# A two-stage attention kernel: more of three fp16 splits moved between ScalarE, VectorE and GpSimd, and PSUM banks of Sx and of k/v alternated one by one

## What is computed

```python
qkv = einsum('bcxy,oc->boxy', gn(x), w_qkv)      # q, k, v: 8 images x 8 heads x 64 x 4096
context = einsum('ndm,nem->nde', softmax(k), v)
content_out = einsum('nde,ndm->nem', context, q)
Sx = einsum('ndxy,xid->nixy', q4, Px)
Yh = einsum('nixy,neiy->nexy', Sx, v4)           # then batch norm over images, rows, columns
Sy = einsum('ndxy,yid->nixy', q4, Py)
out = content_out + einsum('nixy,nexi->nexy', Sy, Yh)
x + einsum('bcxy,oc->boxy', out, w_out) + b_out
```

## Time and profile before

| | us |
|---|---|
| median of 3 runs | 2915.45 (2914.46 to 2922.74) |
| the profiled execution | 2908.83 |
| its span | 2907.0 |
| TensorE busy in the span | 2596.9 (89%) |
| VectorE | 2017.8 (69%) |
| ScalarE | 1689.4 (58%) |
| GpSimd | 1402.7 (48%) |

### The profile page before, as it was taken

The page is one execution under the profiler, slowest core; times in us unless marked ns, Lnnn a source line. Parts: engine busy times, 40 slices in busy tenths (PEclk is TensorE's granted clock), DMA queues, the critical chain, the costliest instruction groups (busy, mean ns, idle before and its releaser), DMA issues. The chain is left out here.

```text
span 2907.0 us, 119666 instructions
## 1 busy us (share of the span) xinstructions
PE 2596.9 (89%) x54900; PEld 2105.4 (72%) x54900; DVE 2017.8 (69%) x3126; ACT 1689.4 (58%) x2984; POOL 1402.7 (48%) x617
## 2 busy tenths in 40 slices
PE   4899999899899999999999996689899898989897
PEld 3787787787687787787777785667676767666674
DVE  7577677677667667667667655787677768677774
ACT  3655655655555565565565564566565656566563
POOL 0424424424434344334344343776766767676761
PEclk9999999999999999999999998799999999999999
DMA  2423523522532542532544335577768777777763
GB/s 99 128 72 82 156 62 88 144 68 75 141 83 68 132 99 69 141 90 68 127 104 119 94 87 121 133 196 194 186 179 229 177 207 172 214 194 197 187 172 109
DMA packets 448615, 382.35 MB, mean 132 GB/s; under 512 B 307312, under 2 KB 374128, under 8 KB 448112
## 3 DMA queue, kind: packets, MB, share of 16 engines
q1 hardware_dynamic: 429680, 341.14, 46.7%
q10 hardware_dynamic: 18432, 33.56, 3.2%
HBM read 205.79 MB, written 168.82 MB: 129 GB/s over the span
## 5 line engine op out<-in xcount | busy, mean ns | idle before, releaser
L843 POOL TENSOR_TENSOR k_f<-k_f,negmax 128x1024 f32<-128x1024 f32 x128 | 303.3, 2397 | 858.7 <-DVE negmax L810 858.7
L456 PE MATMUL bank<-w_hi,x_hi 128*128 128x256 f16 x2048 | 572.0, 279 | 11.0 <-DVE x_lo L735 7.7
L456 PE MATMUL bank<-w_hi,x_lo 128*128 128x256 f16 x2048 | 565.4, 276 | 3.8 <-issue 3.8
L456 PE MATMUL bank<-w_lo,x_hi 128*128 128x256 f16 x2048 | 566.2, 276 | 0.0
L1290 POOL TENSOR_TENSOR x_f<-x_f,ones 128x1024 f32<-128x1024 f32 x127 | 287.2, 2261 | 227.7 <-DMA x_f<-y_scratch 223.2
L1242 DVE TENSOR_TENSOR yb_lo<-x_f,yb_hi 64x1024 f16<-64x1024 f32 x192 | 367.5, 1914 | 31.8 <-ACT yb_hi L1156 28.8
L750 DVE TENSOR_TENSOR v_lo<-bank,v_hi 128x256 f16<-128x256 f32 x512 | 214.0, 421 | 249.5 <-ACT v_hi L598 246.7
L597 ACT ACTIVATE k_f<-bank 128x256 f32<-128x256 f32 x512 | 200.5, 392 | 289.1 <-PE bank L456 287.6
L456 PEld LDWEIGHTS bank<-w_hi,x_hi 128*128 128x128 f16 x2048 | 297.0, 145 | 22.5 <-issue 15.0
L456 PEld LDWEIGHTS bank<-w_lo,x_hi 128*128 128x128 f16 x2048 | 299.7, 146 | 2.3
L456 PEld LDWEIGHTS bank<-w_hi,x_lo 128*128 128x128 f16 x2048 | 297.5, 145 | 2.6
(11 more groups left out here) (152 smaller groups left out, 8312.7 us busy)
## 6 DMA issues: line engine op xcount, KB each, us to landing
y_scratch<-yst SPq DMA_DIRECT2D x256, 256.0 KB, 4.7
x_f<-y_scratch SPq DMA_DIRECT2D x256, 256.0 KB, 6.3
q<-q_scratch SPq DMA_DIRECT2D x256, 256.0 KB, 4.9
x_f<-x SPq DMA_DIRECT2D x64, 512.0 KB, 5.8
q_scratch<-q_hi SPq DMA_DIRECT2D x128, 256.0 KB
q_scratch<-q_lo SPq DMA_DIRECT2D x128, 256.0 KB
x_res<-x SPq DMA_DIRECT2D x128, 256.0 KB, 6.1
out<-x_res ACTq DMA_DIRECT2D x128, 256.0 KB, 4.2
```

The lines of the kernel that those rows point to most:

```text
L456: mm = pe.matmul(outs, lhs[a], rhs[m], start=first and n == 0, stop=last and n == 2, **kw)
L843: pool.tensor_tensor(kk, kk, negmax[:, :].unsqueeze(1).to_broadcast([P, 8, P]), ALU.add).then_inc(shifted, 1)
```

## The change

Three things are moved; the arithmetic stays the same.

1. In the alternating stretches of stage 1, sx and kv alternate one by one.
2. In the split of x, ScalarE casts both channel halves (L576 of the changed kernel in place of L571 and L715); VectorE only subtracts (L721). The last quarter's casts move from behind q 7 to behind sx 0 of head pair 3, and its two subtractions (VectorE, GpSimd) from behind yh 7 to behind sx 2.
3. In stage 2, at head pair 2 `yb_lo` of piece 2 is written by GpSimd too. At head pair 3 piece 2 is split (both halves) behind ro 0 of head pair 3 and no more behind ro 6 and 7 of head pair 2.

```diff
-                for i in range(0, SX, 2):
-                    order += [("sx", hp, i), ("sx", hp, i + 1), ("kv", hp + 1, i), ("kv", hp + 1, i + 1)]
+                for i in range(SX):
+                    order += [("sx", hp, i), ("kv", hp + 1, i)]
...
+            SPLIT_X_HI = {("q", HP - 1, 1): 0, ("q", HP - 1, 3): 1, ("q", HP - 1, 5): 2, ("sx", HP - 1, 0): 3}
+            SPLIT_X_LO = {("yh", HP - 2, 1): 0, ("yh", HP - 2, 3): 1, ("yh", HP - 2, 5): 2, ("sx", HP - 1, 2): 3}
...
                 def split_x(nth, piece):
-                    act.wait_ge(x_norm, nth * 8 + piece * CC + 1)
-                    act.activation(x_hi[:, 0, :, piece * XR:piece * XR + XR, :], x_piece(0, piece),
-                                   ACT.Copy).then_inc(x_hi_a, 1)
+                    for c, done in enumerate((x_hi_a, x_hi_b)):
+                        act.wait_ge(x_norm, nth * 8 + piece * CC + c + 1)
+                        act.activation(x_hi[:, c, :, piece * XR:piece * XR + XR, :], x_piece(c, piece),
+                                       ACT.Copy).then_inc(done, 1)
...
                     s = slice(j * XR, j * XR + XR)
-                    dve.wait_ge(x_norm, nth * 8 + (CC * j + 2))
-                    dve.tensor_copy(x_hi[:, 1, :, s, :], x_piece(1, j)).then_inc(x_hi_b, 1)
+                    dve.wait_ge(x_norm, nth * 8 + (CC * j + 1))
                     dve.wait_ge(x_hi_a, nth * NXC + (j + 1))
...
         LAST_SPLIT = {("ro", 0): ((3, 0),), ("ro", 1): ((3, 1),)}
-
-        LO_DVE = 2 * (YC - 1)
+        LAST_SPLITS = {("ro", 0): ((2, 0), (2, 1)), ("ro", 1): ((3, 0), (3, 1))}
+
+        def on_pool(hp, c):
+            return c == YC - 1 or (hp == 2 and c == YC - 2)
...
                             if i % 2 == 1:
                                 continue
-                            if i < RO - 2:
-                                pe.wait_ge(yb_lo_done, t * LO_DVE + (i + 2))
+                            if on_pool(hp, i // 2):
+                                pe.wait_ge(yb_lo_pool, lows(True, t, i // 2 + 1))
                             else:
-                                pe.wait_ge(yb_lo_pool, t * 2 + 2)
+                                pe.wait_ge(yb_lo_done, lows(False, t, i // 2 + 1))
```

More of the change, by code:

```diff
@@ L816, in turn @@
                                 gn_scale(b + 1)
-                        if kind == "yh" and hp == HP - 2 and i % 2 == 1 and order is not final_turn:
-                            split_x(b + 1, i // 2)
+                        if order is not final_turn and (kind, hp, i) in SPLIT_X_LO:
+                            split_x(b + 1, SPLIT_X_LO[kind, hp, i])
                     if order is final_turn:
@@ L935, in attention_kernel, with lows @@
         LAST_SPLIT = {("ro", 0): ((3, 0),), ("ro", 1): ((3, 1),)}
-        LO_DVE = 2 * (YC - 1)
+        LAST_SPLITS = {("ro", 0): ((2, 0), (2, 1)), ("ro", 1): ((3, 0), (3, 1))}
+        def on_pool(hp, c):
+            return c == YC - 1 or (hp == 2 and c == YC - 2)
+        def lows(pool, t, c=0):
+            pieces = [(k % HP, d) for k in range(t) for d in range(YC)] + [(t % HP, d) for d in range(c)]
+            return 2 * sum(on_pool(*piece) == pool for piece in pieces)
         def splits(b, order, kind, hp, i):
@@ L1273, in turn @@
                         for piece in splits(b, order, kind, hp, i):
-                            if piece[2] < YC - 1:
+                            if not on_pool(piece[1], piece[2]):
                                 split_piece(*piece)
@@ L1311, in _ @@
                 pool.sem_inc(y_norm, 2 * len(DVE_NORM))
-                split_last(0, 0, 2 * YC)
+                split_last(0, 2 * YC)
                 for t in range(1, NT):
```

39 lines of the change are left out of this document (21 added, 18 removed).

## The result

| | before | after |
|---|---|---|
| median, us | 2914.95 (2907.44 to 2922.74, 4 runs) | 2949.64 (2945.67 to 2955.98, 4 runs) |
| ratio, 95% interval | | 1.0121 [1.0086, 1.0155] |
| span of the profiled execution, us | 2907.0 | 2943.9 |

The changed kernel is 34.7 us slower, 1.2%. The two profiled executions stand 36.9 us apart, nearly as the medians do, so they can be used to say where the time lies, as far as one execution of each can (the experiments show how far that is). From the first matmul to the last one of stage 1 it is 1765.9 us before and 1805.8 after, +39.9; from there to TensorE's last matmul it is 1096.2 before and 1093.1 after, -3.1.

A forecast was written before the change was run, and what follows sets the result against it. TensorE's own pace was taken to bound the alternating stretches, the chain behind it the turns, and VectorE's sy_lo waits to hold up stage 2; 10 + 15 + 3 = +28 us on 2915.45 gave 2943 us (8 in 10: 2910 to 2968).

The forecast's parts named there:

- Part 1: Stage 1's 23 alternating stretches: extra changes of tile shape cost +23 us, issue gaps give back 13; +10 us taken.
- the 23 of the sum: Alternating stretches: four more round trips at 0.25 us each, 1.0 us in each of 23 stretches, +23 us before give-back.
- Part 2, first kv: Turns to the next image: first kv waits for VectorE's late x_lo, +1.7 us a turn (+0.9 to +3.1).
- these two marks: At each turn: TensorE waits 3 us or more before the first kv, and x_lo takes over 2 us.
- Part 2, the clock: At each turn: half-speed time after the stall falls on kv instead of sx 6 and 7, +0.5 us (0 to 1.3).
- Part 2, the cast on ScalarE: At the turns: taking the cast from VectorE (1.3 us each) is worth nothing, as the GpSimd, ScalarE, VectorE chain sets the end.
- Part 3: Stage 2: new wait of 1 to 3 us before ro 4, not added in full; +3 us over eight images (-16 to +16).
- the wait before head pair 3 goes: Rival, stage 2: VectorE's splits fall under 1.5 us, sy_lo comes 3.5 us earlier; 2900 us in all, chance 0.09.
- the late piece costs in full: Rival, stage 2: ro 4 waits over 3 us, chain moves 2 us an image, part 1 gives nothing back; 2972 us, chance 0.14.
- the extra time is swallowed: Rival, stage 1: issue gaps give back nearly all of part 1, VectorE finds GpSimd between instructions; 2921 us, chance 0.15.

The follow-up runs named there:

- part 1 alone: Only sx and kv alternating one by one, against the kernel before: 2925.52 us, ratio 1.0050.
- part 2 alone: Only the x split edits (both casts on ScalarE, last quarter's casts behind sx 0, subtractions behind sx 2), against the kernel before: 2935.93 us, ratio 1.0072.
- Part 3 alone: Only the stage 2 edits (GpSimd's extra yb_lo at head pair 2, later piece 2 at head pair 3), against the kernel before: 2916.86 us, ratio 1.0008.

## Why the prediction was right, point by point

Forecast 2943 us (2910 to 2968), measured 2949.64; slower, as forecast. The mechanisms hold, with one exception: the clock at the turns, whose term was too small by a factor of four.

- **Part 1, forecast +10 (0 to +23).** Alone it cost +14.6 us [+9, +20]. The gross cost is 4 x (2 x 2.36 - 4.44) = 1.1 us a stretch, 26 us in 23, close to the 23 of the sum. If all 14.6 us lay in the stretches, 11 would have been given back, where I had taken 13; with the 5 us on the kv at the turns, of which the prediction had nothing, it is more. The profile of one execution can't settle this term: the sum of the 23 stretches is 723.3 us before and 739.6 after (740.6 with part 1 alone), but over the nine profiled kernels that have the order of before in them it runs from 720.9 to 744.6, mean 732.1. The difference of +16.3 between the two profiles is partly chance, and a good part of it is that the kernel before was profiled in a short one.
- **Part 2, first kv, forecast +1.7 us a turn.** Measured +1.42. The steps stand, counted from sx 0 (903.60 before, 920.34 after): end of the casts forecast at 10.6 us, measured 10.5; VectorE's x_lo begins forecast 14.3, measured 14.1. It took 1.79 us, not over 2, and the wait before kv was 1.8 to 3.0 us, not 3 or more: these two marks I had named were missed by little, since GpSimd's running p_lo was nearer its end (933.02 to about 935.15) than I had put it. GpSimd's three p_lo took 7.34 us, 0.95 more than 3 x 2.13: VectorE's x_lo, 1.21 us if the way is free, stood until the first p_lo had ended, and then the second p_lo took 3.14 us. The two engines took turns, by the measure of an instruction each, as with the lock of the Trainium skill, SBUF — State Buffer, section SBUF: two separate sides.
- **Part 2, the clock, forecast +0.5 us a turn: this is the mis-sized term.** Measured +1.90, 13 us in seven turns and not 3.5. I read the half level behind a stall of 4.43 us (2.6 us at 0.53) and took it for a fixed sum that moves from sx to kv. The step that failed is "before, most of that half-speed time lay on sx 6 and 7; now it falls on kv, 0 to 1.3 us more": it didn't move, it got longer. In the mean of the seven turns TensorE stood at the half level for 4.3 us of the sx and 1.05 us of the kv before, and for 4.8 us of the sx and 4.94 of the kv after. The 3.9 us more on kv cost half of themselves, 1.95 us; without that cost the sixteen kv take 21.0 us in both kernels. At the turn shown, TensorE waited 1.20 us at 925.22 and 2.40 at 929.74, the granted clock fell to the half level at about 931.4, before the waits of 0.73 us at 932.12 and 2.77 at 936.38, and stayed there until 941.6: 10.2 us, against 3.4 in the kernel before (915.8 to 919.2). That several stalls in a row are the reason is a reading, and one turn stands against it: at the fifth image of the kernel with part 2 alone the waits were 1.46, 2.12, 1.06 and 3.31 us, and the half level lasted only 3.4 us. Which stalls lengthen it stays open. TensorE's window there:

```profile
934.10:937.50 3.40, 3.33 (x16) 2.71 (x17) 2.91 (x5) 1.35 (x4) 3.40 (x2) 0.50 0.50 154
```
- **Part 2, the cast on ScalarE, forecast worth nothing.** It was worth 6 us where its place was kept. By itself the forecast was off there; in the changed kernel the chain hides it, as said.
- **Part 3, forecast +3 (-16 to +16).** Alone +2 us [-2, +7]. In the changed kernel the wait before ro 4 came in all eight images (0.7 to 5.7 us, 23.2 in all, three of them above the 1 to 3 us of the forecast), and the sy_lo waits before head pair 3 shrank by 17.1 us in all, so most of it isn't added, as forecast. The sy_lo waits are 52.3 us without the three that are GpSimd's, within the forecast of 45 to 65; the 67.3 us of the line have those in them. The profile doesn't name GpSimd's yb_lo (L1319) in any of the eight, as the forecast had it.
- **The rivals.** That the wait before head pair 3 goes needed splits under 1.5 us; they took 2.22 to 2.44 us at the image shown but one (1.47). That the late piece costs in full needed ro 4 to wait over 3 us, which it did in three images of eight, and the chain to move by 2 us an image. Part 3 alone is +2 us for all eight images together. The rival that the extra time is swallowed fell with part 1 alone.

With 16.3 + 9.9 + 13.3 - 3.1 = +36.4 us the terms measured in the two profiles make up their 36.9. By these terms the forecast is some 8 us short: 6 in the stretches and 10 on the clock, less 2 at the first kv and 6 in stage 2, which went the other way. That it is no further off is luck.

## What to carry to other kernels

An instruction that is moved along its own engine should be priced by what that engine was doing at the new place: two casts of 1 us stood free in a wait for GpSimd, and cost 3.3 us seven times once they stood between the two evacuations of a chain. Where matmuls of different tile shapes alternate, two limits pull against each other, the change of shape (0.25 us a round trip) and the arrival of instructions for dense small matmuls, and the best run length has to be measured; here it is one of about 100 matmuls, with four banks of the slower work behind it. When work is moved away from before a wait, look at the next wait of the same engine on the other side: of 50 us taken from the sy_lo waits, 19 came back before the projection and 10 before ro, for yb_lo. And a sum of waits over a whole stage can hide what an edit does: take it over the places that the edit touches.
